# Second attention of a four-layer network: one head per 32-row group of TensorE, mask and maximum in one vector instruction, turned masks by small products

## What is computed

```python
B, T, D = (2, 256, 256)
NH, NKV = (32, 8)
HD = D // NH
...
k = jnp.repeat(k, rep, axis=1)
v = jnp.repeat(v, rep, axis=1)
att = jnp.einsum('bhqd,bhkd->bhqk', q.astype(jnp.float32), k.astype(jnp.float32)) / math.sqrt(HD)
mask = jnp.triu(jnp.ones((seqlen, seqlen), dtype=bool), k=1)
att = jnp.where(mask[None, None, :, :], -jnp.inf, att)
att = jax.nn.softmax(att, axis=-1)
y = jnp.einsum('bhqk,bhkd->bhqd', att, v.astype(jnp.float32)).astype(q.dtype)
y = y.transpose(0, 2, 1, 3).reshape(bsz, seqlen, NH * HD)
return y @ wo
```

## Time and profile before

| | us |
|---|---|
| median of three runs | 1650.41 |
| the profiled execution (its span) | 1650.5 |
| ternary MLP, 1170.50 to 1227.60 | 57.10 |
| second attention, score jobs alone, 1262.97 to 1273.53 | 10.56 |
| second attention, 15 units, 1273.53 to 1447.24 | 173.71 |
| one unit of it, 1330.73 to 1342.45 | 11.72 |
| its last attends and turns, 1447.24 to 1460.50 | 13.26 |

### The profile page before, as it was taken

The page is one execution under the profiler, slowest core; times in us unless marked ns, Lnnn a source line. Parts: engine busy times, 40 slices in busy tenths (PEclk is TensorE's granted clock), DMA queues, the critical chain, the costliest instruction groups (busy, mean ns, idle before and its releaser), DMA issues. The chain is left out here.

```text
span 1650.5 us, 20846 instructions
## 1 busy us (share of the span) xinstructions
PE 1523.2 (92%) x7619; PEld 1074.8 (65%) x7619; DVE 1012.1 (61%) x1903; ACT 674.3 (41%) x1300; POOL 363.2 (22%) x258
## 2 busy tenths in 40 slices
PE   7999999999899868997996899899889999989998
PEld 5788888877767534666885355455664555547887
DVE  6777777721422798245445789898455777744444
ACT  1354555410221240202322699896442555533221
POOL 3100000000401323104005079497661000000000
PEclk9999999999899889989998989899988999999999
DMA  5200000040421400014551022131001333001222
GB/s 189 74 14 19 13 16 16 7 127 22 144 92 56 137 0 1 1 51 166 202 168 52 27 75 99 45 103 64 17 1 29 91 98 84 18 1 53 58 58 64
DMA packets 93906, 105.26 MB, mean 64 GB/s; under 512 B 13909, under 2 KB 77513, under 8 KB 93694
## 3 DMA queue, kind: packets, MB, share of 16 engines
q1 hardware_dynamic: 90750, 95.86, 19.3%
q0 software_dynamic: 3072, 8.30, 1.6%
HBM read 83.39 MB, written 14.55 MB: 59 GB/s over the span
## 5 line engine op out<-in xcount | busy, mean ns | idle before, releaser
L997 POOL TENSOR_TENSOR m_state_c<-m_state,m_c 128x1024 f32<-128x1024 f32 x64 | 153.4, 2399 | 84.9 <-DVE m_state L2896 68.8
L2896 DVE TENSOR_TENSOR_SCAN m_state<-m_decay,psum 128x512 f32<-128x512 f32 x128 | 149.0, 1207 | 14.5 <-POOL m_state_c L997 9.6
L3044 DVE TENSOR_REDUCE a_max_pieces<-psum 128x4 f32<-128x512 f32 (+2 forms) x176 | 107.7, 638 | 52.1 <-PE psum L1764 29.9
L2254 ACT ACTIVATE a_probT<-psum 128x512 f32<-128x512 f32 (+1 forms) x176 | 97.4, 559 | 89.5 <-PE psum L1791 86.0
L1632 PE MATMUL psum<-m_state_c,ident 128*128 128x512 f32 x256 | 121.3, 596 | 3.8 <-POOL m_state_c L997 3.8
L1113 PE MATMUL psum<-ones_bf,ident_bf 128*128 128x512 bf16 x287 | 77.3, 429 | 20.6 <-DVE xn L2354 4.9
L940 POOL TENSOR_TENSOR rstd<-var_eps,half_neg 128x4 f32<-128x4 f32 x18 | 20.2, 1121 | 341.9 <-DVE var_eps L2340 341.7
L2185 ACT ACTIVATE m_b_inputT<-m_dtuT,m_bcT 128x256 f32<-128x256 f32 x218 | 93.1, 496 | 0.6 <-PE psum L1624 0.5
L2605 DVE TENSOR_TENSOR f_h<-f_silu,psum 128x512 f32<-128x512 f32 (+1 forms) x46 | 31.5, 686 | 99.8 <-ACT f_silu L2005 99.1
L2005 ACT ACTIVATE f_silu<-psum 128x512 f32<-128x512 f32 (+1 forms) x46 | 27.5, 597 | 158.6 <-PE psum L1296 158.6
L1624 PEld LDWEIGHTS psum<-ident,m_b_inputT 128*128 128x128 f32 x512 | 62.0, 151 | 42.5 <-DVE m_state L2896 35.2
(11 more groups left out here) (457 smaller groups left out, 3544.9 us busy)
## 6 DMA issues: line engine op xcount, KB each, us to landing
f_fc<-in_L_ffn_fc_w_dram SPq DMA_DIRECT2D x16, 1024.0 KB, 6.1
m_c<-m_c_rows SPq DMA_DIRECT2D x32, 512.0 KB, 3.7
f_share<-f_share_rows SPq DMA_DIRECT2D x32, 256.0 KB, 3.3
f_out_rows<-f_out SPq DMA_DIRECT2D x15, 256.0 KB, 2.2
f_slot_rows<-f_out SPq DMA_DIRECT2D x1, 2560.0 KB, 9.8
f_rows_in<-f_slot_rows SPq DMA_DIRECT2D x10, 256.0 KB, 3.1
wkv<-in_L_attn_Wk_dram SPq DMA_DIRECT2D x16, 128.0 KB, 2.2
wkv<-in_L_attn_Wv_dram SPq DMA_DIRECT2D x16, 128.0 KB, 2.2
```

Of the source, the lines that this page charges most:

```text
L997: pool.tensor_tensor(hc2[c][:], h2[c][:], c_wide[v][:].rearrange("p (b s) -> p b s", b=BATCH), ALU.mult).then_inc(s_hc, 1)
L2254: act.activation(probT3[n % 2][:, PROB3[i]:PROB3[i] + wide], bank[TURNED3[at % 3]][:, 0:wide], ACT.Exp).then_inc(s_exp3, 1)
L2896: ins = dve.tensor_tensor_scan(h2[c][:, b], dec2[c][:, b], bank[4 + 2 * c + b], 0.0, ALU.mult, ALU.add)
L3044: dve.tensor_reduce(max_of3[n % 2][:, int(diagonal), t_, heads[0]:heads[-1] + 1], o, AX.X, ALU.max).then_inc(s_max3, 1)
```

## The change

Each head gets its own group of 32 rows. Rows 32j to 32j+23 of the q stack hold head j's three parts, the same rows of the k stack the group's keys (the same in all four), rows 24 and 25 of each group the two maximum rows and -1. The parts go out to two DRAM buffers (`q_rows3`, `k_rows3`, whose remaining rows are preset to -1 by two early DMAs), and a stack is 2 DMAs. There are 12 jobs in three classes of four heads: 512 columns; 384 and 128; 256. Scores carry no mask: VectorE adds it and takes the maximum by one call (`tensor_tensor_reduce`). A turned product reads 26 rows and is followed by four small bfloat16 products of 32 columns each with 32 rows of the mask. ScalarE copies the turned maxima (`copy_rows`) and SyncE places them by 2 DMAs. `LEAD3` is 8, `attend` stands in four places, the clearing by GpSimd is gone.

```diff
-        JOBS3 = [(3, (j,)) for j in range(REP3)] + [(2, (j,)) for j in range(REP3)] + [(1, (0, 1)), (1, (2, 3)), (0, (0, 1, 2, 3))]
+        PIECES3 = ((3,), (2, 0), (1,))
+        JOBS3 = [(j, PIECES3[c]) for c in range(3) for j in range(REP3)]
...
-        LEAD3, STACKS3 = 3, 4
+        LEAD3, STACKS3 = 8, 4
...
             def stack(n):
...
-                for c, src in enumerate((high, low, high)):
-                    sp.dma_start(q_stack3[u][32 * c:32 * c + 32, :].bitcast(F32), src).then_inc(s_stack3[u], 16)
-                for c, part in enumerate((k_high3, k_high3, k_low3)):
-                    src = part[DH3 * g:DH3 * (g + 1), toks].bitcast(F32)
-                    for j in range(REP3):
-                        at = 32 * c + DH3 * j
-                        sp.dma_start(k_stack3[u][at:at + DH3, j, :].bitcast(F32), src).then_inc(s_stack3[u], 16)
+                sp.dma_start(q_stack3[u][:].bitcast(F32), q_rows3[g, :, :, toks].rearrange("j r c -> (j r) c")).then_inc(s_stack3[u], 16)
+                sp.dma_start(k_stack3[u][:].bitcast(F32), k_rows3[g, :, toks].unsqueeze(0).broadcast_to([REP3, ROWS3, SEQ])).then_inc(s_stack3[u], 16)
+            def place_rows(n):
+                sp.wait_ge(s_mcopied3, COPIED3_0 + n + 1)
+                for c in range(2):
+                    first = MAX_ROW3 + c
+                    sp.dma_start(q_stack3[n % STACKS3][first:first + ROWS3 * (REP3 - 1) + 1:ROWS3, :].bitcast(F32),
+                                 max_rows3[n % 2][REP3 * c:REP3 * (c + 1), :].bitcast(F32)).then_inc(s_mrow3, 16)
...
             for n in range(UNITS3):
...
+                place_rows(n)
+                if n >= 1 and n + 3 < UNITS3:
+                    sp.wait_ge(s_scT3, NJ3 * n)
+                    stack(n + 3)
+                for dst, src, loaded in loads3[2 * n:2 * (n + 1)]:
+                    sp.dma_start(dst, src).then_inc(loaded, 16)
...
             def sum_squares():
-                for i in range(STACKS3 + 2):
-                    clear_stack(i)
...
-                        if n % 2 and STACKS3 + 2 + n // 2 < 3 * STACKS3:
-                            pool.wait_ge(s_ssq, n + 1)
-                            clear_stack(STACKS3 + 2 + n // 2)
...
                 def scores(n, i):
...
-                    mm = pe.matmul(o, q_stack3[u][0:96, t_ * P:(t_ + 1) * P], k_stack3[u][0:96, heads[0]:heads[-1] + 1, s0:s0 + wide],
-                                   start=True, stop=not diagonal)
-                    if diagonal:
-                        mm = pe.matmul(o, ident_bf[:], mask_bf[:].unsqueeze(1).broadcast_to([P, len(heads), P]),
-                                       start=False, stop=True)
+                    for t_ in pieces:
+                        wide = (t_ + 1) * P
+                        mm = pe.matmul(bank[SCORES3[at % 3]][:, column:column + wide], q_stack3[u][r, t_ * P:(t_ + 1) * P],
+                                       k_stack3[u][r, 0:wide], start=True, stop=True)
+                        column += wide
...
                 def turned_scores(n, i):
...
                     if i == 0:
-                        pe.wait_ge(s_mrow3, n + 1)
+                        pe.wait_ge(s_mrow3, 32 * (n + 1))
...
-                    for h, j in enumerate(heads):
-                        pe.matmul(o[:, h], k_stack3[u][:, j, s0:s0 + P], q_stack3[u][:, s0:], start=(h == 0), stop=False,
-                                  skip_group_check=True)
-                    pe.matmul(o[:, :, 0:P], ident_bf[:], maskT_bf[:].unsqueeze(1).broadcast_to([P, len(heads), P]),
-                              start=False, stop=True, skip_group_check=True).then_inc(s_scT3, 1)
+                    for t_ in pieces:
+                        wide, s0 = (t_ + 1) * P, (ST - 1 - t_) * P
+                        o, own = bank[TURNED3[at % 3]][:, column:column + wide], slice(ROWS3 * j, ROWS3 * (j + 1))
+                        pe.matmul(o, k_stack3[u][r, s0:s0 + P], q_stack3[u][r, s0:], start=True, stop=False, skip_group_check=True)
+                        for c in range(ST):
+                            mm = pe.matmul(o[:, ROWS3 * c:ROWS3 * (c + 1)], mask_rows3[own, c, :], ident_bf[own, own], start=False,
+                                           stop=(c == ST - 1), skip_group_check=True)
+                        column += wide
...
-                        if ahead and i == NJ3 - 2:
+                        if ahead and i == NJ3 - 5:
                             turn_max(n + 1)
...
-                        if i in (3, 6) and done:
-                            attend(n - 1, i // 3 - 1)
-                    if done:
-                        attend(n - 1, 2)
-                        attend(n - 1, 3)
+                        if i in (3, 5, 7, 9) and done:
+                            attend(n - 1, (i - 3) // 2)
...
+                def copy_rows(n):
+                    act.wait_ge(s_mturn3, n + 1)
...
+                    act.copy(max_rows3[n % 2][:], bank[7][0:2 * REP3, :]).then_inc(s_mcopied3, 1)
...
                 def maximum(n, i):
...
-                    dve.tensor_reduce(max_of3[n % 2][:, int(diagonal), t_, heads[0]:heads[-1] + 1], o, AX.X, ALU.max).then_inc(s_max3, 1)
+                    for t_ in pieces:
+                        wide = (t_ + 1) * P
+                        ins = dve.tensor_tensor_reduce(masked3[at % 3][:, column:column + wide], bank[SCORES3[at % 3]][:, column:column + wide],
+                                                       mask_wide3[:, SEQ - wide:], 1.0, START, ALU.add, ALU.max,
+                                                       max3[n % 2][:, t_, j:j + 1])
+                        column += wide
```

More of the change, by code:

```diff
@@ L282, in build @@
         x_high0 = Region(here + DM * 4, KT * TOK * 4).take("a0_x_high", [P, KT, TOK], F32R)
-        assert here + DM * 4 + KT * TOK * 4 <= w_odd.end
+        minus_ones = Region(here + DM * 4 + KT * TOK * 4, DM * 4).take("a3_minus_ones", [P, 1, DM])
+        assert here + 2 * DM * 4 + KT * TOK * 4 <= w_odd.end
         slotted(ffn0, w, CAP0, ffn0.routed)
@@ L586, in build @@
         w = work.fresh()
-        probT3 = [w.take(f"a3_probT{u}", [P, WIDE3]) for u in range(2)]
+        probT3 = [w.take(f"a3_probT{u}", [P, REP3, HEAD3]) for u in range(2)]
         q_high3 = w.take("a3_q_high", [P, KT, TOK], F32R)
@@ new lines, in _ @@
+            for b in range(BATCH):
+                sp.wait_ge(s_low3, 2 * b + 2)
+                keep_parts(None, b, s_parts3[b][0])
+                keep_parts(0, b, s_parts3[b][0])
+            for b in range(BATCH):
+                sp.wait_ge(s_parts3[b][0], s_parts3[b][1] + PARTS3)
+                stack(b)
+            for b in range(BATCH):
+                sp.wait_ge(s_low3, 4 + b + 1)
+                keep_parts(1, b, s_parts3[2][0])
+            for n in range(2, STACKS3):
+                stack(n)
@@ L963, in sum_squares @@
             def sum_squares():
-                for i in range(STACKS3 + 2):
-                    clear_stack(i)
+                ch.step(pool.memset(mask_wide3[:], 0.0))
+                ch.step(pool.memset(mask_rows3[:], 0.0))
                 ch.step(pool.memset(sumsq[:], 0.0))
+                ch.sync()
+                ch.step(pool.affine_select(mask_wide3[:, SEQ - P:], mask_wide3[:, SEQ - P:], pattern=[[-1, P]], base=0, channel_multiplier=1,
+                                           compare_op=ALU.is_ge, fill=MASKED))
+                for j in range(REP3):
+                    ch.sync()
+                    rows = mask_rows3[ROWS3 * j:ROWS3 * (j + 1)]
+                    ch.step(pool.affine_select(rows, rows, pattern=[[ROWS3, ST], [-1, P]], base=0, channel_multiplier=1,
+                                               compare_op=ALU.is_ge, fill=MASKED))
+                ch.sync()
                 for b in range(BATCH):
@@ L1801, in attend @@
                             pe.wait_ge(s_pvT3, n)
-                        pe.wait_ge(s_exp3, NJ3 * (n + 1))
+                    pe.wait_ge(s_exp3, NJ3 * n + REP3 * (next(c for c in range(3) if t_ in PIECES3[c]) + 1))
                     for j in range(REP3):
-                        job = next(i for i, (t_, heads) in enumerate(JOBS3) if t_ == ST - 1 - s and j in heads)
-                        wide = (ST - s) * P
-                        at = PROB3[job] + JOBS3[job][1].index(j) * wide
+                        wide = (t_ + 1) * P
                         mm = pe.matmul(bank[6][32 * j:32 * j + 32, s * P:], v_all3[:, b * ST + s, g, :],
-                                       probT3[n % 2][:, at:at + wide], start=(s == 0), stop=(s == ST - 1), tile_position=(0, 32 * j),
-                                       skip_group_check=True)
+                                       probT3[n % 2][:, j, TILE_AT3[t_]:TILE_AT3[t_] + wide], start=(s == 0), stop=(s == ST - 1),
+                                       tile_position=(0, 32 * j), skip_group_check=True)
                     if s == ST - 1:
@@ L2265, in attention3 @@
                             exponent(n, i)
```

(2 more changed lines are left out.)

145 lines of the change are left out of this document (62 added, 83 removed).

## The result

The changed kernel takes 1801.12 us (median of four runs, 1798.86 to 1803.57) where the kernel before took 1650.37: 1.0911 times as long, 95% interval 1.0892 to 1.093. The forecast of 1679 us had the sign; the size is five times as large, and the range (1640 to 1706) misses it by 95 us.

A forecast was written before the change was run, and what follows sets the result against it. The prediction took TensorE's queue to bound the second attention: +1.80 us a unit over 16 units (+28.8), +2.7 before the units and -3.0 in the ternary MLP gave +28.5 on 1650.5, so 1679 us, range 1640 to 1706.

The forecast's parts named there:

- Small products: Second attention, TensorE: 48 more pairs of load and product a unit at 0.035 us each, +1.68 us.
- a boundary: Change to bfloat16 and a partly covered float32 load around a turned product's mask: 0.14 us, five more a unit, +0.70.
- Four masks at 0.24 and the wait for `turn_max` at 0.42: Second attention, TensorE: score masks removed, -0.96 us a unit; wait for the split maxima's `turn_max` goes, -0.42.
- Changes of tile shape: `turn_max` and `turn_back` use the whole array between 32-row products: four more changes, +0.25 us a unit, bounds nothing to 0.5.
- Rows late by DMA: A unit's first turned product waits for the maximum rows placed by SyncE's two DMAs: +0.30 us a unit.
- Rival B: VectorE becomes the bound: its call runs at the scan's pace, 15.8 us a unit, 1716 us; chance 0.08.
- Before the units: 20 score jobs in place of 14 ahead of the first turned product: +4, less 1.3 at the stage's end, +2.7 us.
- Ternary MLP: Without GpSimd's clearing, the 16 silus come closer together: -3.0 us, bounds -3 and 0.
- The detour through DRAM: The parts' way through DRAM buffers, 12 issues before unit 0's and 1's stacks: costed at nothing, 2 us either way.
- A: Rival: products in different row groups overlap, 2.7 us less a unit, kernel faster at 1636 us; chance 0.17.
- C: Rival: the small pairs of load and product cost 0.071 us each, 1707 us; chance 0.12.
- D: Rival: maximum rows' DMAs come 3.1 us late in six or so units, behind other transfers, 1698 us; chance 0.13.

The follow-up runs named there:

- e1_rows128: The changed kernel with the four heads' keys in block form (zeros outside a head's 32 rows), score and turned products reading all 128 rows, small products kept; 1734.1 us.
- e4_warm: The changed kernel with two more products of 128 rows and 512 columns behind each of the 20 score jobs ahead of the units; 1807.0 us.
- b2_few_dmas: The kernel before with VectorE masking and taking maxima in one call, ScalarE copying turned maxima, stacks of 5 DMAs through DRAM buffers, no presets; 1629.09 us.
- e5_rows128_mask: The changed kernel with keys in block form, products reading 128 rows, and one mask product of 128 rows in place of the four small ones; 1657.88 us.
- b0_fills: The kernel before with only two DMAs more at the start, of the size of the changed kernel's presets, their data read by nobody; 1660.11 us.
- e6_lead10: The changed kernel with LEAD3 of 10 in place of 8, so a score and the turned product behind it stand in different row groups; 1749.75 us.

## Why the prediction was wrong

**The step that failed** is the first: "at granted clock 1.00. So this stage is bounded by TensorE's queue: what one unit adds there is paid 16 times". The bound was right, and TensorE's queue stayed the bound; but every duration taken from the rows before was one at 1.00, and the sum carried that clock over to products that read a quarter of the rows. No rival had the clock in it, so the range could not hold the result. A unit went from 11.7 to 20.79 us where +1.80 was forecast. With all rows read, small products and all, it takes 14.65 (e1_rows128), though that kernel has 32 changes of shape a unit more; so at least 6.1 of the 9.1 us are the clock's, and some 8.3 with the 2.1 us of those changes taken off.

**The terms of the sum.** Small products at 0.035 and a boundary at 0.14 gave 0.245 a product; at clock 1.00 the two together took 0.12 (e4_warm, one kind of job), and pairs come 0.025 apart (e1_rows128), so this term was priced too high, and the forecast of "slower" rested on it: with 0.12 it would have been 16 × 0.125 = 2.0 us less a unit, 11.5. Four of the 16 are dearer (0.32 against 0.17 at the low clock), so as an estimate 11.5 to 12.1, against 11.7 before: at clock 1.00 the change would have been worth little either way. The sign came out right for another reason, by luck. Four masks at 0.24 and the wait for `turn_max` at 0.42, 1.38 together, hold as a sum: b2_few_dmas, which drops both, goes from 11.7 to 10.23; no run parts them. Changes of tile shape were taken at 0.06 each (+0.25 for four); those between 32 and 128 rows came to 0.07 at 1.00. Rows late by DMA (+0.30) didn't show: the only such wait of a turned product in the change is ahead of the first unit, and at units of 11.30 (e5_rows128_mask) TensorE is busy 112.93 of 113.00 us.

**VectorE.** The call was put at 1.07 ns a column and 0.14, and its second instruction at 174 ns. In the changed kernel's groups:

```profile
L3064 DVE CUSTOM_DVE_ANT_0 a_masked<-psum,a_mask_wide 128x512 bf16<-128x512 f32 x64 | 43.8, 691 | 85.6 <-PE psum L1779 85.6
...
L3064 DVE DVE_READ_ACCUMULATOR2_ANT a_max<- 128x1 f32 x256 | 21.2, 83 | 0.0
```

The call runs at the reduction's pace, and the read is half as dear. Rival B was out by this.

**Before the units**: +4 for the jobs ahead was right (14.59 against 10.56, +4.0), if partly at a clock of 0.54. **Ternary MLP**: -3.0 was right; the first and last silu stand at 1185.83 and 1227.90, 42.07 us apart where they were 44.96. The detour through DRAM, put at nothing and 2 us either way, let TensorE wait 1.56 us for `a_k_rows`, once.

**Left out altogether** were the two preset DMAs at the start, some 9 us by b0_fills. The prediction counted the DMAs of the second attention and of no other stage, and so put the first score 3 us earlier than before, where it came 5.8 later.

**The rivals.** A's mechanism exists; the reason given against it, that a score and the turned product behind it are always the same head, is just why most of it stayed away, and one number (`LEAD3`) brings 4.1 us a unit of it. That products keep their order, also stated there, the profile doesn't bear out: it shows the next head's score starting ahead of three small products that come before it. C (0.071 a pair) and D were not what happened.

## What to carry to other kernels

A duration in a profile holds for the clock it was taken at; before a product is cut to fewer rows, ask whether the rows that are left keep the granted clock up, and make "the clock falls" a rival with its price, up to the stage's own length once more. Work that uses few rows has to be put so that neighbours in TensorE's queue stand in different row groups (though with that alone, e6_lead10, the clock stayed low and the kernel slower than before), and products of the same row shape belong together, not in turns. And count each DMA of a change where it is issued, at the start of the program too: two presets for a late layer held up the first one.

## What the runs showed that was not expected

- The low clock was left in the midst of work without a gap where products read all rows (e1_rows128, 0.50 to 1.00 between 1330 and 1350 us), although three quarters of the keys' rows held zeros; more than 35 us of such work had gone before.
- Products in two row groups start together when they are neighbours: 16.70 us a unit against 20.79. One can start ahead of products that stand before it in the program.
- A DMA can hold its queue for long: 6.03 us for 1 MB and 3.10 us for 0.25 MB of presets, where an ordinary one takes some 0.57. Here their data held up more than their issue: the next load was issued 1.8 us later than before, and TensorE, without a gap from 30 to 40 us before, was busy 3.90 of these 10 us.
- How many rows are enough was not tried between 32 and 96.
